# First loads reordered over two queues, VectorE's set-up moved later, the softmax in halves and two expert merges in a row: an attention and expert kernel on one core

## The chip, the core and the metric

The kernel runs on one core of a Trainium2 chip. The core has TensorE (PE: matrix products and transposes, results go to PSUM; its weight loads are listed as PEld), VectorE (DVE), ScalarE (ACT), GpSimd (POOL) and SyncE (SP, which here only issues DMAs). Each engine works through its own list of instructions in order, and the lists meet only at semaphores. The metric is the device time of the program in microseconds (us), lower is better.

## The reference, cut to what matters

```python
# x: 64 sequences x 64 tokens x 256
c = einsum('bsi,bij->bsj', x, weight[ids]) + bias[ids]          # 16 categories, one per sequence
x = x + (c + rezero * lora_linear(attention(c)))                # 16 heads of 16, linear position term, softmax
z = lora_out(x, A[lang], B[lang]) + lang_embed[lang]            # 4 languages, rank 16
ys = geglu(z @ Ws1 + bs1) @ Ws2 + bs2                           # shared expert
top2 of (z @ Wr + br) / 1.5 over 12 experts, softmax of the two # router
x = x + ys + sum over top2 of w * (geglu(z @ We1[e] + be1[e]) @ We2[e] + be2[e])
```

`lora_linear(x)` is `x @ W.T + b + (x @ A.T) @ B.T / 8`, for q, k, v and o.

## The kernel before, in words

The 4096 tokens are 32 tiles of 128 rows (two sequences). Three parts follow each other: an attention part over the 32 tiles (to about 373 us), then the shared expert beside the sorting of tokens to experts, then 75 routed tiles of 128 rows. The change touches the first part alone. The order of the instructions on each engine is written out by hand; nothing plans it.

**Start.** SP issues `load_x(0)`, two of the four projection weights (`wT`, L306), the two category weights and biases of tile 0 (`load_condition`, L289 and L291), the other two `wT` (L310), then tile 1 and the first expert weights. ACT issues four small `low` loads (L515) and ten `first_loads` (L517) on one semaphore. PE runs 40 matmuls on ones (`warm`, L1080), the low-rank products of the projections (L1094), 36 more on ones, `condition(0)` (L1115: c = x times the category weight), `router_rows` (L1085), `c_transpose(0)` (L1122), `project_k`, `project_q` (both L1128), `project_v` (L1147), `condition(1)` and `router_products` (L1103, L1104). DVE first waits for all ten first loads (L672), then runs its set-up (L673 to L688: casts, the language masks, the ones in `vD`, scaled biases), then `c_add(0)` (L709), the four `low_rank_weight` (L695, one for each projection, with L701 for the output's) and `lang_routers` (L768).

**One tile i of attention.** PE: `score(i)` (L1161, L1167), `c_transpose(i+1)` (L1122), `o_transpose(i-1)` (L1197), `low_rank(i-2)` (L1218), `project_k` and `project_q` of i+1 (L1128), `output(i-1)` (L1203), `prob_transpose(i)` (L1175), `row_transpose(i-2)` (L1224), `x2_transpose(i-1)` (L1209), `project_v(i+1)` (L1147), `attend(i)` (L1187), `condition(i+2)` (L1115). DVE: `shift(i)` (the row maximum L735 and its subtraction L739), `k_spread(i+1)` (L714), `t_mask(i-2)` (L796, L797), `x2_add(i-1)` (L764), half of `pT_copy` (L745), `v_spread` (L724), `logit_sum` (L802), `normalize` (L751, L753), `c_add(i+2)` (L709). ACT: `cT_copy` (L533), `oT_copy` (L552), `exps(i)` (L544), `q_copy` (L538), the other half of `pT_copy` (L548), `tT_copy`, `x2T_copy`. POOL: the residual sums and `cut_bias`.

**Merges.** The language part `B` and the first layer of each expert are multiplied into one matrix beforehand. An expert has three units of this (`merge`: 8 weight matmuls L1234 and 16 bias matmuls L1238, into PSUM bank 6, copied out by ACT's L523 and L524). A loop of 12 passes takes two tiles and one expert each. In a pass, unit 0 is merged in the middle of the odd tile (`merge_a`: behind `o_transpose`, in the place of `low_rank`, which then comes behind the projections), unit 1 at the end of the odd tile and unit 2 at the end of the even tile (`merge_b`). Tiles 1 and 2, ahead of the loop, each end with a merge of the shared expert. Tiles 27 to 31, behind it, have none. `logit_consts` (L785, L787) runs once on DVE between tiles 2 and 3.

## Time and profile before

| quantity | value |
|---|---|
| median of 3 runs | 844.94 us (844.64 to 846.51) |
| the profiled execution's own time | 845.6 us |
| its span, first to last instruction | 843.5 us |
| mean granted TensorE clock | 0.992 of full speed |
| PE busy | 811.8 us (96%) |
| DVE busy | 546.8 us (65%) |
| ACT busy | 282.0 us (33%) |
| POOL busy | 406.1 us (48%) |

Times in rows count from the span's start. A timeline row gives the start in us, the length in us, engine and source line, operation, target and sources, how many instructions are put together, and in square brackets how long the engine was idle before it and what it had waited for. PE and PEld overlap: a weight load for the next matmul runs while the present one streams. The engines of one queue run in the written order, so a row that starts late holds up all that stands behind it.

### The profile page before, as it was taken

The page shows a single profiled execution, that of the slowest core. Times are in us where ns is not written, and L with a number is a line of the kernel's source. Part 1 is how long each engine was busy: PE and PEld are TensorE (multiplying, and loading weights), DVE is VectorE, ACT ScalarE, POOL GpSimd, SP SyncE. Part 2 cuts the span into 40 slices and gives each one's busy share as a digit, 9 for nine tenths or more (in the row PEclk, how much of TensorE's full clock was granted, in tenths as well). Part 3 has the DMA queues.
Part 4 walks back from the last instruction along what each step waited for, and adds up shares of the span by engine and source line. Part 5 has one row for each costly group of instructions (what it writes and reads, how often), then busy time and mean ns, then how long its engine had stood idle before and what let it go on. Part 6 is the DMA issues. An engine that isn't in the chain of part 4 may idle for free. (4 is left out here: it accounts for less than half of the span.)

```text
span 843.5 us, 27449 instructions
## 1 busy us (share of the span) xinstructions
PE 811.8 (96%) x9371; PEld 675.0 (80%) x9372; DVE 546.8 (65%) x1231; ACT 282.0 (33%) x783; POOL 406.1 (48%) x511
## 2 busy tenths in 40 slices
PE   6899999999999999979999999999999999999995
PEld 5778888888888888856777888888888888888884
DVE  2586666666666667758887567676676666666662
ACT  0333333333333333433332333232323333332330
POOL 2133333444334444210101277777777777777762
PEclk9999999999999999999999999999999999999998
DMA  9445555555555553103863323222232323232222
GB/s 277 130 137 173 171 161 156 157 167 156 160 168 154 153 158 90 46 2 139 251 209 125 125 34 39 35 35 37 33 39 32 39 33 39 33 38 34 35 34 25
DMA packets 49004, 85.59 MB, mean 101 GB/s; under 512 B 7266, under 2 KB 27554, under 8 KB 48834
## 3 DMA queue, kind: packets, MB, share of 16 engines
q1 hardware_dynamic: 33634, 68.76, 26.2%
q0 software_dynamic: 13888, 15.13, 13.4%
q10 hardware_dynamic: 1440, 1.16, 0.5%
q8 instruction: 23, 0.38, 0.2%
q14 instruction: 19, 0.16, 0.1%
HBM read 68.48 MB, written 16.55 MB: 101 GB/s over the span
## 5 line engine op out<-in xcount | busy, mean ns | idle before, releaser
L1429 PE MATMUL ps<-arena,stage 128*128 x900 | 206.6, 379 | 0.0
L1429 PEld LDWEIGHTS ps<-arena,stage 128*128 128x128 f32 x900 | 165.3, 190 | 19.4
L480 POOL DMA_INDIRECT out_dram<-stage,to_row x75 | 120.6, 1608 | 74.9 <-DVE stage L1040 63.4
L636 ACT ACTIVATE stage<-ps 128x384 f32<-128x384 f32 x150 | 65.4, 488 | 241.6 <-PE ps L1416 241.6
L1416 PE MATMUL ps<-token_rows,token_rows_T 64*128 64x128 f32 x1800 | 129.2, 272 | 0.0
L1416 PEld LDWEIGHTS ps<-token_rows,token_rows_T 64*128 64x128 f32 x1800 | 118.8, 189 | 1.7
L472 POOL DMA_INDIRECT token_rows<-gated_rows,from_row x75 | 75.0, 1000 | 64.6 <-DVE to_row L923 42.0
L388 POOL TENSOR_TENSOR arena<-arena 128x256 f32<-128x256 f32 x32 | 23.3, 729 | 148.7 <-DVE arena L764 148.7
L1014 DVE COPY token_rows<-ps 128x128 f32<-128x128 f32 x75 | 21.8, 291 | 109.6 <-PE ps L1398 109.6
L1024 DVE TENSOR_TENSOR stage<-ps,stage 128x384 f32<-128x384 f32 x150 | 75.8, 547 | 1.8 <-ACT stage L636 1.8
L735 DVE TENSOR_REDUCE arena<-ps 128x16 f32<-128x1024 f32 x32 | 39.2, 1224 | 49.4 <-PE ps L1167 49.2
L1128 PE MATMUL ps<-arena 128*128 128x128 f32 x512 | 66.9, 285 | 1.3 <-ACT arena L533 1.3
L1128 PEld LDWEIGHTS ps<-arena 128*128 128x128 f32 x512 | 61.2, 196 | 4.5 <-issue 2.4
L1410 PE MATMUL ps<-token_rows,token_rows_T 64*128 64x256 bf16 x450 | 62.1, 273 | 0.0
L1327 PE MATMUL ps<-ws,stage 128*128 128x256 f32 x256 | 59.2, 384 | 0.4 <-ACT token_rows_T L560 0.4
L1327 PEld LDWEIGHTS ps<-ws,stage 128*128 128x128 f32 x256 | 47.4, 190 | 10.3 <-issue 4.0
L523 ACT COPY w_merged<-ps 128x256 f32 (+1 forms) x38 | 14.1, 372 | 120.4 <-PE ps L1238 120.4
L267 DVE COPY token_rows_T<-w_merged 128x256 f32 x75 | 46.6, 621 | 0.7 <-issue 0.7
L544 ACT ACTIVATE arena<-arena 128x1024 f32<-128x1024 f32 x32 | 34.0, 1061 | 35.8 <-DVE arena L739 35.8
L1016 DVE TENSOR_SCALAR token_rows<-ps,consts 128x128 bf16<-128x128 f32 x150 | 45.0, 341 | 0.0
L487 POOL COPY token_rows_T<-w_bias 128x384 bf16 x75 | 42.6, 568 | 1.0 <-issue 0.8
L724 DVE TENSOR_TENSOR arena<-ps,arena 64x256 f32<-64x256 f32 x64 | 27.1, 423 | 24.6 <-PE ps L1147 24.2
(170 smaller groups left out, 1482.1 us busy)
## 6 DMA issues: line engine op xcount, KB each, us to landing
stage<-in_we_dram SPq DMA_DIRECT2D x36, 512.0 KB, 4.2
arena<-in_cond_w_dram SPq DMA_DIRECT2D x64, 256.0 KB, 2.9
arena<-in_we_dram SPq DMA_DIRECT2D x12, 768.0 KB, 4.9
arena<-in_x_both_dram SPq DMA_DIRECT2D x32, 256.0 KB, 2.6
arena<-in_L_cond_bias_dram SPq DMA_DIRECT2D x64, 64.0 KB, 2.7
out_dram<-arena SPq DMA_DIRECT2D x32, 128.0 KB, 1.7
be_bc<-in_be_rows_dram SPq DMA_DIRECT2D x13, 192.0 KB, 2.7
gated_rows<-token_rows POOLq DMA_DIRECT2D x2, 1152.0 KB, 10.2
```

The source lines that it names most:

```text
L267: copy(w1x[s % 2][:, j * CW:(j + 1) * CW], w1m[:, ds(e * (NJ * CW) + j * CW, CW)]).then_inc(w1x_ok[j], 1)
L472: pool.indirect_dma_start(s_row[s], None, gated_rows, bass.IndirectOffsetOnAxis(from_row[:, t:t + 1], 0)).then_inc(d_row[s], 16)
L480: pool.indirect_dma_start(out_rows, bass.IndirectOffsetOnAxis(to_row[:, t:t + 1], 0), y_sb[t % YR], None, compute_op=ALU.add).then_inc(d_a ...
L487: nc.gpsimd.tensor_copy(w1bx[t % 2].bitcast(bf16), w1b[:, ds(e * (NJ * P), NJ * P)]).then_inc(w1bx_ok, 1)
L636: nc.scalar.activation(g_sb[hf].rearrange("p (j n) -> p j n", n=P), first_out[1][:, :, hf, :], ACT.Gelu).then_inc(g_ok, 1)
L1016: last = V.tensor_scalar(s_langT[s % 2][:, hf * P:(hf + 1) * P], ps[:, 7, P:2 * P], col["half"][:, hf:hf + 1], None, ALU.mult)
L1024: V.tensor_tensor(actT_sb[s % 2][:, hf, :].rearrange("p (j n) -> p j n", n=P), first_out[0][:, :, hf, :], g_sb[hf].rearrange("p (j n) -> p ...
L1128: last = mm(ps[:, bank, at + m * P:at + (m + 1) * P], wm[w][:, k, m * P:(m + 1) * P], cT[:, k, :], start=(k == 0), stop=(k == KC - 1))
L1327: last = mm(ps[:, 4 + v, half * D:(half + 1) * D], sh_aT[half][:, k, v * P:(v + 1) * P], ws2[:, k, :], start=(k == 0), stop=(k == HS // P ...
L1410: mm(first_out[g][:, j].rearrange("p h n -> p (h n)"), w1bx[s % 2].bitcast(bf16)[64 * g:64 * g + 64, at], s_langT[s % 2][64 * g:64 * g + 6 ...
L1416: last = mm(first_out[g][:, j, hf, :], w1x[s % 2][64 * g:64 * g + 64, j * CW + hf * P:j * CW + (hf + 1) * P], s_rowT[s % 2][64 * g:64 * g ...
L1429: last = mm(ps[:, 4 + s % 2, 0:D], actT_sb[s % 2][:, hf, j * P:(j + 1) * P], arena[:, ds(e * E2 + (NJ * hf + j) * D, D)], start=(hf == 0 a ...
```

## The change

- **Loads.** SP: only the transposed half of tile 0's x, the K weight, the category weights of tile 0 (both value loads first, then both weights, then both biases), the Q weight, the position table (`alibi`), the V weight, tile 1, the output weight, and so on. ACT: four `low`, then the first 132 columns of `consts`, `small`, `bo`, `bv`, the other half of x, and six loads for later (`rest_loads`). The one semaphore of the first loads becomes three (`d_first`, `d_near`, `d_rest`), with one of its own for the half of x. The projections come in the order K, Q, V, output.
- **DVE's set-up.** DVE begins with the K weight and `c_add(0)`. `lang_setup` (the output's weight, `tri`, the language masks, `lang_routers`) stands in tile 0 behind `k_spread(1)`; `langB` is built behind tile 0. On PE `router_rows` moves into tile 0 and `router_products` behind it; 8 `warm` matmuls stand behind `condition(0)`.
- **Waits of other queues.** POOL's `residual(0)` now waits for `s_first` (the scaled `bo`) and comes before the copy of the language masks; SP waits for the pair (`merge_ps`) before it loads units 0 and 1 of the next expert.
- **Softmax in halves.** `shift` and `exps` are each made of two halves of 512 columns, and `prob_transpose` waits for each half.
- **Merges.** Units 0 and 1 are merged together at the end of the odd tile (`merge_pair`, the weights in bank 6, the biases in bank 7), copied by ACT in `pair_bias_copy` and `pair_copy`. The middle of the odd tile has `low_rank` again; in the even tile `o_transpose` waits for `pair_bias` and `low_rank` stands behind the projections. The number of matmuls stays.

```diff
-        first_loads = [
-            (consts[:, :], a["consts"]), (small, a["small"]), (ali_f, a["alibi"]),
-            (aT.rearrange("p c l n -> p (c l n)"), a["lora_aT"]), (a_rows, a["lora_a"]), (ba[:, :, :].rearrange("p c n -> p (c n)"), a["lora_ba"]),
-            (lang_i[:, :], a["lang_of"]), (lang_b[:, :], a["lang_rows"]), (bv_half, a["bv_half"]), (bo_bc, a["bo_rows"])]
-        ALL_FIRST = 16 * len(first_loads)
-        PROJECTIONS = (1, 2, 0, 3)
+        near_loads = [(bo_bc, a["bo_rows"]), (bv_half, a["bv_half"])]
+        rest_loads = [
+            (ba[:, :, :].rearrange("p c n -> p (c n)"), a["lora_ba"]), (consts[:, EARLY:], a["consts"][:, EARLY:]),
+            (lang_i[:, :], a["lang_of"]), (lang_b[:, :], a["lang_rows"]),
+            (a_rows, a["lora_a"]), (aT.rearrange("p c l n -> p (c l n)"), a["lora_aT"])]
+        FIRST, NEAR, REST = 16 * 2, 16 * (len(near_loads) + 1), 16 * len(rest_loads)
+        PROJECTIONS = (1, 0, 2, 3)
...
-            load_x(0, 0)
-            for n in PROJECTIONS[0:2]:
-                sp.dma_start(wm[n].rearrange("p c n -> p (c n)"), a["wT"][n]).then_inc(d_wT[n], 16)
+            sp.dma_start(x_in[0][:, D:2 * D], a["x_both"][0, :, D:2 * D]).then_inc(d_x[0], 16)
+            sp.dma_start(wm[PROJECTIONS[0]].rearrange("p c n -> p (c n)"), a["wT"][PROJECTIONS[0]]
+                         ).then_inc(d_wT[PROJECTIONS[0]], 16)
             sp.wait_ge(d_cat, 16)
             load_condition(0, 0)
-            for n in PROJECTIONS[2:]:
-                sp.dma_start(wm[n].rearrange("p c n -> p (c n)"), a["wT"][n]).then_inc(d_wT[n], 16)
+            n = PROJECTIONS[1]
+            sp.dma_start(wm[n].rearrange("p c n -> p (c n)"), a["wT"][n]).then_inc(d_wT[n], 16)
+            sp.dma_start(ali_f, a["alibi"]).then_inc(d_near, 16)
+            n = PROJECTIONS[2]
+            sp.dma_start(wm[n].rearrange("p c n -> p (c n)"), a["wT"][n]).then_inc(d_wT[n], 16)
+            load_tile(1, True)
+            n = PROJECTIONS[3]
+            sp.dma_start(wm[n].rearrange("p c n -> p (c n)"), a["wT"][n]).then_inc(d_wT[n], 16)
             sp.dma_start(bs2_bc[:, :], a["bs2_rows"]).then_inc(d_bs2, 16)
-            load_tile(1, True)
             for j in range(NJS):
...
-            for dst, src in first_loads:
-                act.dma_start(dst, src).then_inc(d_first, 16)
-
-            def merge_copy(n, j, at_col, summed=None):
+            act.dma_start(consts[:, 0:EARLY], a["consts"][:, 0:EARLY]).then_inc(d_first, 16)
+            act.dma_start(small, a["small"]).then_inc(d_first, 16)
+            for dst, src in near_loads:
+                act.dma_start(dst, src).then_inc(d_near, 16)
+            act.dma_start(x_in[0][:, 0:D], a["x_both"][0, :, 0:D]).then_inc(d_first_x, 16)
+            for dst, src in rest_loads:
+                act.dma_start(dst, src).then_inc(d_rest, 16)
+
+            def merge_copy(n, j, at_col):
                 act.wait_ge(merge_ps, n + 1)
-                if summed is not None:
-                    act.wait_ge(l_sum, summed)
                 copy(w1m[:, ds(at_col, CW)], ps[:, 6, 0:CW])
                 copy(l_ps[:, j * P:(j + 1) * P], ps[:, 6, CW:CW + P]).then_inc(merge_sb, 1)
 
-
-            act.wait_ge(s_sp1, 1)
-            copy(wr[0:NLR + NLANG, :], ps[0:NLR + NLANG, 6, 0:NE]).then_inc(s_sp1c, 1)
-            act.wait_ge(s_hot, 1)
+            def pair_bias_copy(e):
+                act.wait_ge(merge_ps, 2 * e + 3)
+                act.wait_ge(l_sum, e + 1)
+                copy(l_ps[:, 0:2 * P], ps[:, 7, D:D + 2 * P]).then_inc(pair_bias, 1)
+
+            def pair_copy(e):
+                copy(w1m[:, ds(e * (NJ * CW), 2 * CW)], ps[:, 6, 0:2 * CW]).then_inc(merge_sb, 1)
...
             def exps(i):
-                act.wait_ge(shift_sb, i + 1)
-                nc.scalar.activation(probs, probs, ACT.Exp).then_inc(prob_sb, 1)
+                for half in range(2):
+                    act.wait_ge(shift_sb, 2 * i + (half + 1))
+                    part = probs[:, 512 * half:512 * half + 512]
+                    nc.scalar.activation(part, part, ACT.Exp).then_inc(prob_sb, 1)
...
+                tile_steps(i)
+                pair_bias_copy(e)
+                tile_steps(i + 1, pair_of=e, merged=dict(n=2 * e + 3, j=2, at_col=e * (NJ * CW) + 2 * CW))
...
-            dve.wait_ge(d_first, ALL_FIRST)
-            V.tensor_copy(ali, ali_f).then_inc(s_const, 1)
-            V.tensor_copy(tri_b[:, :], col["tri"]).then_inc(s_const, 1)
-            V.tensor_copy(lang_tmp, lang_b[:, :])
-            link(V.tensor_copy(lang_f, lang_i[:, :]))
-            link(V.tensor_scalar(lang_tmp, lang_tmp, col["lang_row"], col["one_row"], ALU.is_equal, ALU.add))
-            for hf in range(2):
-                V.tensor_scalar(langB[:, hf, :], lang_tmp, col["half"][:, hf:hf + 1], None, ALU.mult)
-            for lang in range(NLANG):
-                V.tensor_scalar(lang_hot[:, :, lang], lang_f, float(lang), None, ALU.is_equal)
-            dve.wait_ge(s_zero, 3)
-            for s in range(2):
-                for h in range(2):
-                    V.tensor_copy(vD[s][:, :, :, 32 + h],
-                                  col["kv"][:, h:h + 1].unsqueeze(2).to_broadcast([P, 2, 8]))
-            V.tensor_scalar(bq_quarter, bq_col, 0.25, None, ALU.mult)
-            V.tensor_scalar(bo_rz, bo_bc, rz, None, ALU.mult).then_inc(s_hot, 1)
-            dve.wait_ge(s_hot, 1)
...
             def shift(i):
                 dve.wait_ge(s_ps, i + 1)
-                V.tensor_reduce(smax.rearrange("p (g h) -> p g h", g=4), scores, AX.X, ALU.max).then_inc(max_sb, 1)
-                dve.wait_ge(max_sb, i + 1)
                 if not isinstance(i, int) or i > 0:
                     dve.wait_ge(pT_ps, 2 * i)
-                V.tensor_tensor(probs.rearrange("p (g h k) -> p g h k", g=4, k=S), scores,
-                                smax.rearrange("p (g h) -> p g h", g=4).unsqueeze(3).to_broadcast([P, 4, 4, S]),
-                                ALU.subtract).then_inc(shift_sb, 1)
+                for half in range(2):
+                    banks = slice(2 * half, 2 * half + 2)
+                    top = smax[:, 8 * half:8 * half + 8].rearrange("p (g h) -> p g h", g=2)
+                    V.tensor_reduce(top, scores[:, banks], AX.X, ALU.max).then_inc(max_sb, 1)
+                    dve.wait_ge(max_sb, 2 * i + (half + 1))
+                    V.tensor_tensor(probs[:, 512 * half:512 * half + 512].rearrange("p (g h k) -> p g h k", g=2, k=S),
+                                    scores[:, banks], top.unsqueeze(3).to_broadcast([P, 2, 4, S]),
+                                    ALU.subtract).then_inc(shift_sb, 1)
...
+            def lang_setup():
+                low_rank_weight(3, PROJECTIONS[3])
+                dve.wait_ge(d_rest, REST)
+                V.tensor_copy(tri_b[:, :], col["tri"]).then_inc(s_const, 1)
+                V.tensor_copy(lang_tmp, lang_b[:, :])
+                link(V.tensor_copy(lang_f, lang_i[:, :]))
+                for lang in range(NLANG):
+                    ins = V.tensor_scalar(lang_hot[:, :, lang], lang_f, float(lang), None, ALU.is_equal)
+                ins.then_inc(s_hot, 1)
+                dve.wait_ge(s_hot, 1)
+                lang_routers()
...
+            low_rank_weight(0, PROJECTIONS[0])
             c_add(0, False)
-            for at, n in enumerate(PROJECTIONS):
-                low_rank_weight(at, n)
-            lang_routers()
+            low_rank_weight(1, PROJECTIONS[1])
+            dve.wait_ge(d_first, FIRST)
+            V.tensor_scalar(bq_quarter, bq_col, 0.25, None, ALU.mult).then_inc(s_first, 1)
             k_spread(0)
+            low_rank_weight(2, PROJECTIONS[2])
+            dve.wait_ge(d_near, NEAR)
+            V.tensor_copy(ali, ali_f).then_inc(s_const, 1)
+            V.tensor_scalar(bo_rz, bo_bc, rz, None, ALU.mult).then_inc(s_first, 1)
+            dve.wait_ge(s_zero, 3)
+            for s in range(2):
+                for h in range(2):
+                    V.tensor_copy(vD[s][:, :, :, 32 + h],
+                                  col["kv"][:, h:h + 1].unsqueeze(2).to_broadcast([P, 2, 8]))
             v_spread(0, False)
             c_add(1, True)
-            tile_steps(0, False)
+            tile_steps(0, False, lang_setup)
             router_consts()
+            link(V.tensor_scalar(lang_tmp, lang_tmp, col["lang_row"], col["one_row"], ALU.is_equal, ALU.add))
+            for hf in range(2):
+                V.tensor_scalar(langB[:, hf, :], lang_tmp, col["half"][:, hf:hf + 1], None, ALU.mult)
             tile_steps(1, True)
...
             def prob_transpose(i):
-                pe.wait_ge(prob_sb, i + 1)
                 for n in range(8):
+                    if n % 4 == 0:
+                        pe.wait_ge(prob_sb, 2 * i + (n // 4 + 1))
                     last = tr(ps[:, n // 4, (n % 4) * P:(n % 4 + 1) * P], probs[:, n * P:(n + 1) * P], ident)
...
+            def merge_pair(e, i):
+                for j in range(2):
+                    pe.wait_ge(d_stage[j], 16 * e + 32)
+                pe.wait_ge(tT_sb, i - 1)
+                pe.wait_ge(merge_sb, 2 * e + 2)
+                pe.wait_ge(x2T_sb, i)
+                for j in range(2):
+                    merge_weights(j, j * CW)
+                for j in range(2):
+                    last = merge_biases(j, 7, D + j * P)
...
                 score(i)
                 if one_more:
                     c_transpose(i + 1)
+                if after_pair is not None:
+                    pe.wait_ge(pair_bias, after_pair + 1)
                 if not isinstance(i, int) or i > 0:
                     o_transpose(i - 1)
-                if merge_a:
-                    merge(*merge_a, rows=i - 2 if late else None)
-                elif late:
+                if late and after_pair is None:
                     low_rank(i - 2, merged)
                 if one_more:
                     project_k(i + 1)
                     project_q(i + 1)
-                if merge_a:
+                if late and after_pair is not None:
                     low_rank(i - 2, merged)
+                between()
...
             warm(36)
             condition(0, False)
-            router_rows()
+            warm(8)
+            pe.wait_ge(d_first, FIRST)
             c_transpose(0)
             pe.wait_ge(s_mrgc, 1)
             project_k(0)
+            pe.wait_ge(s_mrgc, 2)
+            project_q(0)
             pe.wait_ge(s_mrgc, 3)
-            project_q(0)
             project_v(0)
             condition(1, True)
-            pe.wait_ge(s_mrgc, 4)
+            pe.wait_ge(s_const, 1)
+            tile_steps(0, False, 0, between=router_rows)
             pe.wait_ge(s_sp1c, 1)
             pe.wait_ge(s_zero, 4)
             router_products()
-            tile_steps(0, False, 0)
-            pe.wait_ge(ar_sb, 1)
-            tile_steps(1, True, 0, merge_b=(0, 0, 16))
-            tile_steps(2, False, 1, merge_b=(1, 1, 16))
+            pe.wait_ge(s_mrgc, 4)
+            tile_steps(1, True, 0, single=(0, 0, 16))
+            tile_steps(2, False, 1, single=(1, 1, 16))
             with pe.Fori(0, NE) as e:
                 i = 2 * e + 3
-                tile_steps(i, True, 3 * e + 3, merge_a=(3 * e + 2, 0, 16 * e + 32), merge_b=(3 * e + 3, 1, 16 * e + 32))
-                tile_steps(i + 1, False, 3 * e + 4, merge_b=(3 * e + 4, 2, 16 * e + 16))
+                tile_steps(i, True, 2 * e + 2, pair=e)
+                tile_steps(i + 1, False, 2 * e + 3, single=(2 * e + 3, 2, 16 * e + 16), after_pair=e)
             for i in range(2 * NE + 3, NT):
                 tile_steps(i, i % 2 == 1, n_merge)
```

## Rows read from the trace of the kernel before

**Rows 1.** Windows of loop tiles: stretch, length, busy PE, PEld, DVE, ACT, POOL, clock, DMA.

```profile
180.44:190.91 10.47, 10.27 (x163) 8.70 (x160) 6.85 (x14) 3.88 (x10) 2.33 (x4) 1.00 0.63 210
190.91:202.74 11.83, 11.80 (x183) 9.69 (x183) 7.03 (x14) 4.43 (x12) 6.81 (x9) 1.00 0.40 119
```

**Rows 2.** Timeline of the start, chain to the first score of tile 0.

```profile
7.39 3.47 PE L1080 MATMUL ps<-ones_b 128*128 128x128 bf16 x36
...
11.78 1.09 PE L1115 MATMUL ps<-arena 128*64 128x256 f32 x8 [0.92 <-DMA arena<-in_cond_w_dram]
...
14.28 0.36 DVE L673 CAST arena<-arena 128x384 bf16<-128x384 f32 x1 [14.15 <-DMA arena<-in_bo_rows_dram]
...
16.78 0.42 DVE L709 TENSOR_TENSOR arena<-ps,arena 128x256 f32<-128x256 f32 x1
...
17.13 2.47 DVE L695 SCALAR_TENSOR_TENSOR arena<-ps,arena 128x512 f32<-128x512 f32 x4
...
18.56 3.75 PE L1128 MATMUL ps<-arena 128*128 128x128 f32 x16 [0.61 <-ACT arena L533]
...
22.25 1.85 PE L1147 MATMUL ps<-arena 128*64 128x128 f32 x16
...
24.91 0.64 PE L1103 MATMUL ps<-arena 64*128 64x48 f32 x4
...
25.83 0.32 PE L1161 MATMUL ps<-arena 2*64 2x256 bf16 x8
```

**Rows 3.** Windows of the start, same columns: the last numbers are clock, DMA share, GB/s.

```profile
17.20:20.00 2.80, 2.12 (x9) 1.75 (x10) 2.77 (x6) 0.37 (x1) 2.06 (x3) 0.50 0.99 372
```

**Rows 4.** DMA issues from 6.50 to 6.70 us (KB, median us to landing).

```profile
arena<-in_wT_dram SPq DMA_DIRECT2D x1, 256.0 KB, 6.4
```

**Rows 5.** Timeline of tile 0 and the start of tile 1, at full clock.

```profile
26.56 0.44 PE L1122 MATMUL ps<-consts,arena 128*128 128x128 f32 x2
...
27.46 2.05 PE L1128 MATMUL ps<-arena 128*128 128x128 f32 x16 [0.46 <-ACT arena L533]
...
31.37 1.15 PE L1147 MATMUL ps<-arena 128*64 128x128 f32 x16
...
32.29 1.13 PE L1187 MATMUL ps<-arena 128*64 128x34 f32 x32
...
35.11 0.32 PE L1161 MATMUL ps<-arena 2*64 2x256 bf16 x8 [0.80 <-DVE arena L778]
```

**Rows 6.** Timeline of one even tile of the loop.

```profile
181.32 1.22 DVE L735 TENSOR_REDUCE arena<-ps 128x16 f32<-128x1024 f32 x1 [1.61 <-PE ps L1167]
...
181.66 0.60 PE L1218 MATMUL ps<-arena 128*128 128x112 f32 x4
...
182.06 1.86 PEld L1128 LDWEIGHTS ps<-arena 128*128 128x128 f32 x16
...
182.67 1.23 DVE L739 TENSOR_TENSOR arena<-ps,arena 128x1024 f32<-128x1024 f32 x1
...
185.02 0.42 DVE L764 TENSOR_TENSOR arena<-ps,arena 128x256 f32<-128x256 f32 x1
185.04 0.86 PEld L1175 LDWEIGHTS ps<-consts,arena 128*128 128x128 f32 x8 [0.46 <-ACT arena L544]
...
185.97 0.25 PEld L1209 LDWEIGHTS ps<-consts,arena 128*128 128x128 f32 x2
```

**Rows 7.** DVE and ACT by form: duration ns min/median/max of 512 and of 1024 columns.

```profile
L745 DVE COPY arena<-ps x32: 690/691/692, 31.5 to 366.4; 128x512 f32<-128x512 f32 x32
...
L544 ACT ACTIVATE arena<-arena x32: 1056/1057/1070, 29.2 to 364.1; 128x1024 f32<-128x1024 f32 x32
```

**Rows 8.** Timeline of tile 3, the first of the loop.

```profile
59.58 1.22 DVE L735 TENSOR_REDUCE arena<-ps 128x16 f32<-128x1024 f32 x1 [0.23 <-DVE logit_consts L787]
...
63.31 1.09 PE L1175 MATMUL ps<-consts,arena 128*128 128x128 f32 x8 [1.70 <-ACT arena L544]
```

**Rows 9.** Timeline of tile 31, the last of the attention part.

```profile
365.23 1.09 PE L1175 MATMUL ps<-consts,arena 128*128 128x128 f32 x8 [1.75 <-ACT arena L544]
```

102 lines of the change are left out of this document (60 added, 42 removed).

## The prediction, made before the changed kernel was run

> **What bounds the kernel now.** I read the busy shares first: PE is busy for 96% of the span (the table above), so time can only come from where PE is idle, where it runs at the lower clock, or where its own order of work has gaps. The windows of single loop tiles come next. In the even tile PE is busy 10.27 of 10.47 us, in the odd one 11.80 of 11.83 [rows 1]: both together hold 0.23 us of idleness in 22.30 us, and 12 passes 2.8 us. This is all that the softmax and the merges can win in the loop, small gaps between groups aside. The start is different: tile 0 is scored at 25.83 us [rows 2], and PE has not done much by then. So I followed the chain to this score, then tiles 0, 1 and 3, where the change adds work to DVE, then one pass, then the end. Sums are made in the profiled execution's time, 845.6 us, which is 0.7 above the median of 844.94.
>
> **The start.** The chain is condition(0), c_add, c_transpose, the projections, condition(1), score [rows 2].
> - Condition(0) waited 0.92 us for a category weight behind the last warm matmul, which ended at 10.86. The new order puts the half of x and one projection weight ahead of it, in place of all of x and two weights, and issues the second category weight right behind the first. It should be there by about 9, so condition(0) runs from 10.86 to 11.95: 0.9 won.
> - DVE's c_add started at 16.78, though condition(0) was done at 12.87: DVE waited for the last first load until 14.28 and then worked 2.5 us on its set-up. Now only the K weight stands before it (2.47 / 4 = 0.62 us, done early), so c_add runs at 12.0 to 12.45. PE spends 8 warm matmuls (8 x 3.47 / 36 = 0.77) beside it, so c_transpose starts at 12.75. At full clock project_k follows c_transpose by 0.90 [rows 5], at 13.65, and both projections take 2.05, to 15.7.
> - V now waits: k_spread(0) until 15.6, the V weight 0.62, project_v at 16.3 for 1.15 [rows 5], condition(1) 1.1 with some overlap, and the score at 18.45. The small pieces of DVE's set-up that stay (position table, scaled `bo`, ones) are about 1.2 us and lie beside project_v. Weights: the third one was issued at 6.6 and landed 6.4 us later, at 13.0 [rows 4]; Q now takes about its place in the bytes, with slightly fewer ahead, and is wanted at 12.45. That is close, and worth 0.5 us if late.
> - The clock: between 17.2 and 20.0 us it was granted at 0.50, the 1.2 GHz level [rows 3], after PE had done next to nothing between 12.87 and 17.2, the end of c_add. There the projections took 3.75 us where they take 2.05 warm, project_v 1.85 where it takes 1.15 [rows 2, 5]. The new gaps are 0.5 to 0.7 us each, far from the 4.3 us of before, so I take the upper level throughout. This is 2.4 us of the sum; if the clock falls all the same, it is lost.
> - The router products (from 24.91 to the score at 25.83, 0.9 us) leave the start.
> Together the score of tile 0 comes at 18.45 in place of 25.83: **7.4 us won**.
>
> **Tiles 0 and 1 give back.** In tile 0 DVE has, from the score on: scores ready 0.9, shift 2.95, k_spread 0.87, the output's weight 0.62 and its scaling 0.5, 7 of 17 set-up instructions (7/17 of 2.5 = 1.0), the routers 0.25, pT_copy 0.69: 7.7. attend needed 6.46 (32.29 - 25.83), now 7.7. Behind it stood 2.82 us to the next score, 0.80 of it a wait for the router constants [rows 5]; now the router products stand there, for about the same. Tile 0: 9.28 becomes 10.5, **1.2 lost**. Everything that queues behind the new waits on DVE (pT_copy, v_spread, normalize) is in this. In tile 1 the constants and langB delay shift by about 0.35, of which 0.1 comes through; tile 2 gives 0.1. The loads of tile 2 wait for POOL's residual(0), now behind the scaled `bo` at about 17.4, against 16.8 before: they are wanted 9 us later.
>
> **Halves.** 512 columns take DVE 0.691 us [rows 7], 1024 take 1.225: a fixed 0.157 us for each instruction. Two more of them, and one more wait for a maximum (0.13 between maximum and subtraction in the loop [rows 6]), less the overlap of one instruction with the next (0.09), lengthen DVE's chain: 1.35 + 1.23 becomes 2.93, **0.35 us more** in each tile. The Trainium skill's "VectorE: DVE Perf Modes" (TRN2 errata) advises tiles of at least 512 elements so that the fixed latency amortizes; halves are just that size. By the rule DVE's chain would not grow; the rows say 23% of a half is fixed. With the rule's reading the total would be some 1.5 us lower. A half of the exponentials takes between 0.53 (half of 1.057) and 0.69 us [rows 7], say 0.6, so the first is ready 1.5 us sooner than all of them were and the second 0.1, and PE's wait before prob_transpose (0.46 on its weight load [rows 6], some 0.25 of real time) goes. What is late next is x2_add. Its end was 4.12 behind the maximum's start (181.32 to 185.44), now 4.47, so x2_transpose can start at 185.85 where it started at 185.97 [rows 6]. **An even tile wins 0.12, not 0.25.**
>
> **Merges in the loop.** The matmuls stay. The odd tile loses the merge in its middle and gets it at its end, where one transition between groups less is worth about 0.1. But that merge covered the exponentials (odd: no idleness) and the cT copy. Odd tile: x2_transpose stood 5.5 into the tile without its merge, and DVE's longer chain also gives 5.55: 11.83 becomes 11.78. Even tile: project_k waits for the cT copy until 182.06 whether low_rank stands ahead of it (from 181.66, about 0.44 until the next group) or not [rows 6], so moving low_rank behind adds 0.44, less the 0.26 of the wait for the exponentials, now covered: 10.47 becomes 10.65. A pass: +0.12. With 12 even and 11 odd tiles (tile 3 is below): **1.5 lost**. Bounds for a pass: -0.33 (all idleness and the transition) to +1.14 (0.44, and 0.35 on both tiles, with nothing won). I take a value near the lower end, since the chain above is made of rows. ACT's copy of the pair's biases (0.37) has 0.9 us until o_transpose. The loads of units 0 and 1 are issued a tile later than before and wanted a pass later.
>
> **Tile 3.** logit_consts holds DVE until 59.58, long after the scores are ready. The merge in the middle lay under this; PE still waited 1.70 [rows 8]. Now the merge comes after: x2_transpose starts at 59.58 + 4.47 + 0.05 = 64.1 (before: 63.31 and the 0.93 from prob_transpose to it in rows 6, 64.2), then 4.7 to the tile's end plus the 1.6 of the second merge: **1.45 lost**. The cover is gone, the stall is not.
>
> **The end.** Tiles 27 to 30 win 0.1 each. In tile 31 PE waits 1.75 for the exponentials [rows 9]; the first four transposes now fall into that wait and the second half is ready a little sooner: 0.6. **1.0 won**. What follows hangs on this chain and shifts as a whole.
>
> **Sum.** 7.4 - 1.2 - 1.5 - 1.45 + 1.0 = 4.2 us: 845.6 becomes 841.4, or 840.7 at the median's level.
>
> **Two queues.** ACT already issued ten loads, so the second queue is not new; what changes is order and bytes. "DMA: Bandwidth & Descriptors" of the Trainium skill (Rules for kernel authors) says that spreading loads over queues gives no bandwidth. The gain above counts none from it; nothing in the traces here can part the two.
>
> **Rivals.**
> - *The clock falls at the start.* The two gaps before and after the projections join if Q or V land late. For it: at 12.87 a gap did it. Against: PE is busy for most of 10.9 to 18.5. It costs 2.4: 843.1.
> - *The loop wins.* If x2_add turns out to be no limit and the pair saves two transitions, a pass wins 0.2: 12 x 0.32 better than forecast, 836.9. For it: the margins are 0.1 us. Against: in rows 6 DVE's chain is that close to PE.
> - *The loop loses, slower in all.* The place is the even tile's projections and the x2_transpose of both tiles: without the merge in the middle nothing lies beside cT copy and softmax, and the longer DVE chain comes through whole. At the upper bound, 1.14 a pass, the loop costs 13.7 in place of 1.5: 852.9. It makes the change slower by over 0.2% from 0.62 a pass on. Against: PE has 5.5 us of its own work before x2_transpose. A part of it, 0.4 a pass, gives 844.1.
> - *The change does not do what it says:* condition(0) still finds its weight late and Q's weight at 13.0. That takes back 1.4: 842.1.
>
> **How the numbers follow.** A measurement here tells 0.2%, 1.7 us. Forecast 840.7 with its near neighbours (839 to 842): 0.50. Loads not earlier: 0.06, faster. Loop wins: 0.15, faster. Cold start: 0.11, on the edge at 843.1; I give 0.04 to faster and 0.07 to same. Loop loses in part: 0.11, same. Loop loses in full: 0.07, slower. Faster 0.75, same 0.18, slower 0.07. The range from 836.5 to 844.5 leaves out the slower case and a part of the partial one.
>
> **What would show it.** Right: score(0) near 18.5 and the clock at 1.00 from 11 us on; attend(0) waiting for DVE; score(1) near 29; tile 3 near 15 us long; a pass of 22.4; in the even tile a wait for ACT before project_k; no wait before prob_transpose. Wrong: a clock of 0.50 before 25 us; a pass under 22.1 or over 22.7; PE waiting for `pair_bias`; a shift of DVE longer than 2.95.

## The result, and the profile after

The changed kernel takes 834.83 us (median of 4 runs, 834.17 to 835.57) where the one before takes 845.04 (4 runs): a ratio of 0.9874, with a 95% interval of 0.9861 to 0.9888. That is 10.2 us faster. The forecast was 840.7, 4.2 us faster, with a range down to 836.5, so the direction was right and the forecast size was less than half of what came. The profiled execution took 834.26 us, with a span of 832.0, 11.5 below the span of before.

Busy time of each engine, from the page of the changed kernel:

```profile
span 832.0 us, 27568 instructions
...
PE 802.4 (96%) x9379; PEld 677.4 (81%) x9380; DVE 551.5 (66%) x1295; ACT 285.6 (34%) x791; POOL 406.1 (49%) x511
```

DVE is busy for 4.7 us more than before; with the halves alone (run h_only below) it is 3.6 us more. PE is busy for 9.4 us less with 8 more matmuls. Some 2.1 us of this are the matmuls on ones, the projections and project_v of the start (rows below). For the rest, busy time is what the overlapping records cover together, and it gets smaller when they lie closer.

The start of the changed kernel (timeline: start, length, engine and line, operation, count, in brackets the idle time before). L1114 are the matmuls on ones, L1149 condition, L714 c_add, L1162 the projections, L1181 project_v, L1195 the score.

```profile
6.78 2.18 PE L1114 MATMUL ps<-ones_b 128*128 128x128 bf16 x36
...
8.90 1.09 PE L1149 MATMUL ps<-arena 128*64 128x256 f32 x8
...
10.99 0.42 DVE L714 TENSOR_TENSOR arena<-ps,arena 128x256 f32<-128x256 f32 x1 [3.42 <-DMA arena<-in_L_cond_bias_dram]
...
12.52 3.38 PE L1162 MATMUL ps<-arena 128*128 128x128 f32 x16 [0.55 <-DVE arena L700]
...
15.83 1.38 PE L1181 MATMUL ps<-arena 128*64 128x128 f32 x16
...
18.00 0.32 PE L1195 MATMUL ps<-arena 2*64 2x256 bf16 x8
```

They answer to rows 2. Condition(0) starts 2.9 us sooner, c_add 5.8 sooner and the score 7.8 sooner. The matmuls on ones took 2.18 us where they took 3.47 for the same 36. The projections still took 3.38 us, at a granted clock of 0.50 from about 13 to 16 us.

Windows of an odd and an even tile of the loop and of tile 3 (stretch, length, busy PE, PEld, DVE, ACT, POOL, clock, DMA share, GB/s), against rows 1:

```profile
161.01:172.29 11.28, 11.28 (x184) 9.98 (x185) 6.97 (x16) 4.08 (x11) 6.77 (x9) 1.00 0.45 152
172.29:182.95 10.66, 10.25 (x164) 8.76 (x160) 7.07 (x16) 4.43 (x12) 2.33 (x4) 1.00 0.59 184
48.00:62.54 14.54, 11.94 (x188) 9.89 (x184) 10.90 (x19) 4.04 (x11) 6.34 (x9) 1.00 0.34 108
```

The odd tile got shorter by 0.55 us and the even one longer by 0.19, as had been worked out for the even one (10.65). Taken as means of eleven passes, a pass went from 22.27 to 21.92. From the starts of the scores in both timelines the 11.5 us divide as follows (positive: won).

| stretch | forecast | measured |
|---|---|---|
| start to score(0) | 7.4 | 7.8 |
| tile 0 | -1.2 | -0.9 |
| tiles 1 and 2 | 0 | 0.4 |
| tile 3 | -1.45 | -0.9 |
| score(4) to score(27) | -1.5 | 3.7 |
| score(27) to the end | 1.0 | 1.4 |

The forecast of this sum was 4.2 us and it came to 11.5. The loop carries 5.2 of the missing 7.3 us; the other five lines came out 0.3 to 0.55 better each.

### The profile page after: what moved, and what is told of

Read it like the earlier page. It is cut to its first block, busy times and chain, and to the rows that moved or that the text cites. A ratio compares the mean times of both kernels' runs of the same rounds, so it can differ in the third digit from the quotient of the medians.

```text
span 832.0 us, 27568 instructions
## 1 busy us (share of the span) xinstructions
PE 802.4 (96%) x9379; PEld 677.4 (81%) x9380; DVE 551.5 (66%) x1295; ACT 285.6 (34%) x791; POOL 406.1 (49%) x511
## 4 chain that ended last, share of the span: by engine, by line
PE 92%; DVE 3%; issue 1%; ACT 1%; DMA 1%; SPq 1%; POOL 0%; DVEq 0%
PE ps L1490 23%; PE ps L1477 12%; PE ps L1162 7%; PE ps L1388 7%; PE ps L1181 4%; PE ps L1471 4%; PE ps L1264 4%; PE ps L1210 3%; PE ps L1222 3%; PE ps L1238 3%; PE ps L1149 3%; PE ps L1377 3%; PE ps L1270 2%; PE ps L1458 2%; PE ps L1201 2%; PE ps L1253 2%
## 5 line engine op out<-in xcount | busy, mean ns | idle before, releaser
L745 DVE TENSOR_REDUCE arena<-ps 128x8 f32<-128x512 f32 x64 | 43.8, 685 | 64.4 <-PE ps L1201 64.1
L1162 PE MATMUL ps<-arena 128*128 128x128 f32 x512 | 66.5, 284 | 4.2 <-ACT arena L552 3.6
L1162 PEld LDWEIGHTS ps<-arena 128*128 128x128 f32 x512 | 60.8, 195 | 7.7 <-ACT arena L552 7.0
L565 ACT ACTIVATE arena<-arena 128x512 f32<-128x512 f32 x64 | 40.4, 631 | 38.2 <-DVE arena L747 37.1
L747 DVE TENSOR_TENSOR arena<-ps,arena 128x512 f32<-128x512 f32 x64 | 44.2, 691 | 2.2
L1471 PEld LDWEIGHTS ps<-token_rows,token_rows_T 64*128 64x128 bf16 x450 | 22.2, 95 | 24.9 <-issue 24.9
```

What stands on the lines that cost most here:

```text
L747: V.tensor_tensor(probs[:, 512 * half:512 * half + 512].rearrange("p (g h k) -> p g h k", g=2, k=S), scores[:, banks], top.unsqueeze(3).to ...
L1162: last = mm(ps[:, bank, at + m * P:at + (m + 1) * P], wm[w][:, k, m * P:(m + 1) * P], cT[:, k, :], start=(k == 0), stop=(k == KC - 1))
L1471: mm(first_out[g][:, j].rearrange("p h n -> p (h n)"), w1bx[s % 2].bitcast(bf16)[64 * g:64 * g + 64, at], s_langT[s % 2][64 * g:64 * g + 6 ...
```

## The experiments

All times are medians; a ratio is to the kernel before on the same chip, and comparisons between sets go by ratios, because the kernel before took 845.8, 846.0, 846.7 and 847.3 us in the four sets. Starts of scores come from the timelines. A trace shows one execution, and not always a typical one, which matters where the clock fell in it.

**1. The three parts alone.** Each is the kernel before with one part of the change: `shift`, `exps` and `prob_transpose` in halves; the pair with its copies, waits and counts; or everything else.

```diff
-                V.tensor_reduce(smax..., scores, AX.X, ALU.max)
+                for half in range(2):
+                    V.tensor_reduce(top, scores[:, banks], AX.X, ALU.max)
```

> The kernel before with the softmax in halves and nothing else. Theory A (in the loop PE only loses its wait for the exponentials, and x2_add is no limit, since DVE's chain grows by 0.16 us and not by 0.35): the even tile falls from 10.47 to about 10.22, the odd one stays at 11.83, tiles 27 to 30 win 0.15 to 0.2 each and tile 31 0.6: about 4 us in all, 841. Theory B (the loop's gain in the changed kernel comes from the pair, halves give the 0.12 an even tile that was forecast): 2.4 us, 842.6.

Measured: 839.16 us, ratio 0.9918 (0.9905 to 0.9932), 6.6 us won. The two tiles of a pass:

```profile
155.84:166.06 10.22, 10.05 (x164) 8.80 (x160) 6.96 (x16) 4.11 (x12) 2.33 (x4) 1.00 0.69 212
166.06:177.87 11.81, 11.81 (x185) 9.66 (x186) 7.26 (x16) 4.51 (x13) 6.79 (x9) 1.00 0.44 122
```

The even tile is where theory A put it, at 10.22, but the whole is 2.6 us more than the 4 of theory A. Its trace is 6.0 us shorter than the one before: 3.1 from score(4) to score(27), 1.4 in tiles 0 to 3, where theory A counted nothing, and 1.5 behind score(27). DVE's part of this even tile:

```profile
156.81 0.69 DVE L742 TENSOR_REDUCE arena<-ps 128x8 f32<-128x512 f32 x1 [1.71 <-PE ps L1172]
...
157.54 0.69 DVE L744 TENSOR_TENSOR arena<-ps,arena 128x512 f32<-128x512 f32 x1
...
158.15 0.68 DVE L742 TENSOR_REDUCE arena<-ps 128x8 f32<-128x512 f32 x1
...
158.86 0.69 DVE L744 TENSOR_TENSOR arena<-ps,arena 128x512 f32<-128x512 f32 x1
...
160.56 0.41 DVE L769 TENSOR_TENSOR arena<-ps,arena 128x256 f32<-128x256 f32 x1
```

The four pieces take 2.74 us (156.81 to 159.55), against 2.58 before (181.32 to 183.90 in rows 6). The 0.13 between maximum and subtraction became 0.04 and 0.03. x2_add ends 4.16 after the first maximum, against 4.12 before.

That 0.13 was never a cost of the two operations. In the kernel before it is 0.13 to 0.14 in the 24 tiles of the loop, but 0.03 to 0.04 in the eight tiles outside it, as here in tile 0:

```profile
26.72 1.23 DVE L735 TENSOR_REDUCE arena<-ps 128x16 f32<-128x1024 f32 x1 [1.27 <-PE ps L1167]
27.98 1.23 DVE L739 TENSOR_TENSOR arena<-ps,arena 128x1024 f32<-128x1024 f32 x1
```

With the halves it is 0.03 to 0.04 in all 32 tiles. The code of the halves puts the wait for `pT_ps` ahead of the first maximum, where it stood between maximum and subtraction. That this is what took the 0.10 is likely but was not run by itself.

```diff
-                tile_steps(i, True, 3 * e + 3, merge_a=(3 * e + 2, 0, ...), merge_b=(3 * e + 3, 1, ...))
-                tile_steps(i + 1, False, 3 * e + 4, merge_b=(3 * e + 4, 2, ...))
+                tile_steps(i, True, 2 * e + 2, pair=e)
+                tile_steps(i + 1, False, 2 * e + 3, single=(2 * e + 3, 2, ...), after_pair=e)
```

> The kernel before with units 0 and 1 merged as a pair at the end of the odd tile and nothing else. Theory A (a second merge behind the first costs 1.3 us in place of 1.6, but the odd tile now waits for the exponentials, 0.26, and the even one for the cT copy): a pass of about 22.2 for 22.31, and tile 3 about 1 us longer: 844.5, within 1 us of before. Theory B (the pair carries the loop's gain): a pass of 21.95, 3.5 us in all, 841.5. Theory C, the forecast's own sizes (+0.12 a pass with halves, more without): 847 or slower.

Measured: 848.51 us (10 runs, 847.6 to 850.7), ratio 1.0033 (1.0022 to 1.0044): 2.8 us slower. A pass:

```profile
161.97:172.64 10.67, 10.26 (x163) 8.77 (x160) 6.93 (x14) 4.22 (x11) 2.32 (x4) 1.00 0.55 185
172.64:184.32 11.68, 11.63 (x185) 9.98 (x185) 6.84 (x14) 3.87 (x10) 6.77 (x9) 1.00 0.47 145
```

As means of eleven passes the odd tile is 11.64, the even one 10.65 and a pass 22.28, against 22.27 before, so the pair alone does nothing in the loop. Tile 3 takes 14.92 for 13.62. This explains 1.3 of the 2.8 us. The time is that of theory C (847 or slower), but not by its reason, since the pass did not grow; theory A had the loop and tile 3 right and the time wrong. The profiled execution was the slowest of the ten (850.66). It shows the clock at 0.50 around 372 us and 1.1 us more behind score(27), and a start 2.5 us later in front of which nothing was changed. How much of the rest the clock makes is not settled.

```diff
-            dve.wait_ge(d_first, ALL_FIRST)
-            (the set-up, then c_add(0), the four weights, lang_routers)
+            low_rank_weight(0, PROJECTIONS[0])
+            c_add(0, False)
+            (as in the change)
```

> The kernel before with the new order of the loads and of DVE's set-up and nothing else. Both theories: score(1) at about 28 for 35.1, tiles 1 to 31 as before: 7 us, 838. If the start's gain were given back later or were a matter of the clock's phase at the start, it would be under 5 us, 840 or more, with a wide spread of the times.

Measured: 839.09 us, ratio 0.9923 (0.991 to 0.9937), 6.7 us won; score(0) at 18.72, score(1) at 28.62. The start keeps what it wins. But not all else is as before: from score(4) to score(27) this kernel is 0.9 us faster too. The first eight matmuls of each pass take 0.32 us, where they take 0.46 in the kernel before, and the odd tile is 11.70 for 11.79; why is not shown. The three parts alone sum to 6.6 - 2.8 + 6.7 = 10.5 us, about what they make together.

**2. Order inside the pair.**

```diff
                 for j in range(2):
                     merge_weights(j, j * CW)
-                for j in range(2):
                     last = merge_biases(j, 7, D + j * P)
```

> The changed kernel with the matmuls of a pair in the order weights, biases, weights, biases in place of weights, weights, biases, biases. The same matmuls, two more changes of the matmul's tile shape in each pass. If such a change costs PE about 0.15 us (a matmul row of 8 weights starts the next group after 1.02 us alone and 0.86 as a second one), a pass is 0.3 longer, 12 passes 3.5 us: 838.3. If changes of shape are free and the pass is shorter for another reason (no wait, the start of the loop body): no difference, 834.8.

Measured: 838.8 us, ratio 0.9913, against 0.9874 of the changed kernel (0.9883 when run again): about 3 us slower. As means of eleven passes, a pass went from 21.92 to 22.21, all of it in the odd tile (11.28 to 11.56), which is 3.1 us from score(4) to score(27). The merges of the changed kernel and, below, of this one (timeline, PE):

```profile
169.40 1.95 PE L1264 MATMUL ps<-stage,ba 128*64 128x256 f32 x16
...
171.28 1.08 PE L1270 MATMUL ps<-stage,ba 128*32 128x128 f32 x32
...
172.29 0.32 PE L1195 MATMUL ps<-arena 2*64 2x256 bf16 x8
```

```profile
149.62 1.08 PE L1264 MATMUL ps<-stage,ba 128*64 128x256 f32 x8
150.63 0.64 PE L1270 MATMUL ps<-stage,ba 128*32 128x128 f32 x16
151.21 1.08 PE L1264 MATMUL ps<-stage,ba 128*64 128x256 f32 x8
152.22 0.64 PE L1270 MATMUL ps<-stage,ba 128*32 128x128 f32 x16
152.79 0.32 PE L1195 MATMUL ps<-arena 2*64 2x256 bf16 x8
```

The same 48 matmuls take 2.89 us in one order (169.40 to 172.29) and 3.17 in the other. Two more changes from one kind of matmul to the other cost 0.28, 0.14 each. The two kinds differ in the tile's shape, in the columns that they stream (256 and 128) and in the PSUM bank that they write. From weights to biases the bank is not what counts: in the kernel before both kinds write bank 6, and the two groups together take the same 1.59 us. Shape and columns were not parted.

**3. The changed kernel with one part less, and again.** The kernels of this set ran beside each other.

> The changed kernel once more, as the measure for the kernels of this set: about 10.5 us under the kernel before, 835 on a chip where that takes 845.5. In its trace passes of 21.94 and tile 3 of 14.5.

Measured: 836.19 us, ratio 0.9883 (0.9867 to 0.99). Its tile 3 took 16.09 us where the first profile had 14.54. Windows inside it:

```profile
52.00:54.00 2.00, 0.62 (x3) 0.19 (x1) 1.63 (x4) 0.12 (x1) 1.15 (x2) 1.00 0.03 12
54.00:56.00 2.00, 0.77 (x5) 0.54 (x6) 1.97 (x6) 1.31 (x4) 0.00 (x0) 1.00 0.01 4
56.00:58.00 2.00, 2.00 (x15) 1.55 (x16) 1.27 (x4) 1.42 (x5) 1.19 (x2) 0.72 0.00 0
58.00:60.00 2.00, 2.00 (x34) 2.00 (x32) 0.83 (x2) 0.00 (x0) 1.13 (x3) 0.50 0.61 139
```

PE is busy for 1.39 of 4 us while it waits for the late exponentials, then the clock falls to the 1.2 GHz level from about 57 to 60 us, and the tile is 1.55 us longer. The first profile shows the same gap (PE busy for 1.40 of the 4 us) and a clock of 1.00 throughout the tile. So the gap brings the fall in some executions and not in others: of the seven profiles of kernels with the pair and with `logit_consts` in one piece five have it in tile 3, and of the nine others none.

```diff
-                tile_steps(i, True, 2 * e + 2, pair=e)
+                tile_steps(i, True, 3 * e + 3, merge_a=(3 * e + 2, 0, ...), merge_b=(3 * e + 3, 1, ...))
```

> The changed kernel with the three merges where they were before (start and halves kept). Theory A' (from the traces of the single parts: with halves alone a pass is 22.03 and tile 3 13.2, with all three 21.94 and 14.5; the pair wins 12 x 0.09 and gives 1.3 back at tile 3): no difference to the changed kernel, within 0.5 us. Theory B' (the times, in which the pair alone made the kernel before 2.8 us slower, hold here too): 2 us or more faster than the changed kernel.

Measured: 832.51 us, ratio 0.984 (0.9826 to 0.9855): 3.7 us faster than the changed kernel beside it. Theory A' missed, theory B' held. A pass and tile 3:

```profile
148.71:158.97 10.26, 10.05 (x163) 8.80 (x160) 6.97 (x16) 4.14 (x12) 2.33 (x4) 1.00 0.68 217
158.97:170.68 11.71, 11.71 (x185) 9.62 (x185) 7.26 (x16) 4.47 (x13) 6.81 (x9) 1.00 0.40 116
47.61:60.85 13.24, 12.36 (x187) 9.51 (x184) 10.90 (x19) 4.58 (x13) 6.32 (x9) 1.00 0.33 98
```

The passes are equal, 21.97 here and 21.94 with the pair (21.92 for both as means). At score(4) this kernel is already 3.3 us ahead (60.85 for 64.17), 2.85 of them from tile 3: 1.3 because the merge lies inside the wait again (13.24 for 14.54) and 1.55 because the clock did not fall.

```diff
-                for half in range(2):
+                V.tensor_reduce(smax..., scores, AX.X, ALU.max)      (exps and prob_transpose likewise)
```

> The changed kernel with the softmax whole (start and pair kept). Theory A': a pass goes back to 22.28, the odd tile waits 0.3 for the exponentials; tiles 27 to 31 give back 1.2; 12 x 0.34 + 1.2 and some tenths for tiles 1 to 3: about 5.8 us slower than the changed kernel, near 841. If the halves' worth in the kernel before (6.6) was there because nothing else covered the exponentials, and the pair had taken a part of it: 3 us or less.

Measured: 842.2 us (839.2 to 844.3), ratio 0.9943 (0.9926 to 0.9961): 6.0 us slower, as expected. The halves are worth about the same with the pair as without, but in another tile. Here the odd tile is 11.56 and the even one 10.66, as means; with the halves they are 11.28 and 10.65. Without the pair the halves shorten the even tile (10.49 to 10.21) and leave the odd one alone (11.79 and 11.81).

```diff
+            logit_consts(0)
             tile_steps(2, False)
-            logit_consts()
+            logit_consts(NT // 2)
```

> The changed kernel with logit_consts cut in two: its first half (2.5 us on DVE) between tiles 1 and 2, its second between tiles 2 and 3. Theory A' (tile 3 takes 14.5 and not 11.3 since DVE comes to its scores 3.4 us late and the merge that lay beside this is now behind it): each half makes the shift 0.9 us late at most, PE has 5.3 us of its own work before x2_transpose and DVE 4.2, so tile 3 falls to 11.3 to 11.6 and tile 2 grows by 0.2 at most: 3 us faster than the changed kernel. If the cover is not the cause (a first pass of a loop is slow for another reason): no gain.

Measured: 832.27 us, ratio 0.9839 (0.9821 to 0.9858): 3.9 us faster than the changed kernel. Tile 3, at full clock:

```profile
48.53:60.57 12.04, 11.73 (x188) 9.98 (x185) 8.46 (x17) 4.04 (x11) 5.63 (x9) 1.00 0.38 124
```

It falls to 12.04, not quite to the 11.3 to 11.6 that were expected, and tile 2 grows from 9.98 to 10.43. By the traces this is 2.1 us against an execution of the changed kernel without the fall of the clock, and 3.6 against the one with it. So the long wait at tile 3, with the fall that it brings in some executions, is what makes the pair cost: the pair's 3.7 us come back when the wait is cut short with the pair in place.

**4. What the start's gain is made of.**

```diff
-            (loads as changed)
+            (both halves of x, two projection weights, category weights and biases, two projection weights; ACT: consts in two pieces, ..., bo last)
```

> The changed kernel with the loads issued in the order of before (both halves of x, two projection weights, category weights and biases by turns, alibi third and bo last on ACT's queue, consts whole at once in two pieces); DVE's set-up, softmax and merges as changed. Theory 1 (the start's gain comes mostly from c_add no longer standing behind DVE's set-up and the last load): condition(0) waits for the category weight until about 11.8 and c_add runs at 13, score(0) at about 20 for 18.0: 2 us slower than the changed kernel, 837.5 or so. Theory 2 (the order of the loads carries it): score(0) at 22 or later, 4 us slower or more.

Measured: 835.76 us (835.1 to 839.3), ratio 0.987 (0.9851 to 0.9889), the same as the changed kernel. By the median both theories missed. The edit differs from its description in one point: inside `load_condition` the order stayed that of the change (both weights, then both biases), so this order was not taken back. The one profiled execution took 839.32, with the clock at 0.50 from 12 to 18 us and again in tile 3:

```profile
11.40 1.59 PE L1149 MATMUL ps<-arena 128*64 128x256 f32 x8 [2.90 <-DMA arena<-in_cond_w_dram]
...
14.94 3.75 PE L1162 MATMUL ps<-arena 128*128 128x128 f32 x16 [0.55 <-ACT arena L552]
```

Here condition(0) starts 2.5 us later than in the changed kernel, and score(0), at 20.59, 2.6 later, as theory 1 had it. The other three executions, between 835.1 and 836.2, have no trace; their mean granted clocks (0.996, 0.996, 0.992) are above the 0.990 of the profiled one and reach above the 0.992 to 0.994 of the changed kernel in the second set. So fewer falls of the clock may hide a cost of the old order, and this stays open.

```diff
+            dve.wait_ge(d_rest, REST)
+            dve.wait_ge(d_near, NEAR)
             low_rank_weight(0, PROJECTIONS[0])
```

> The changed kernel, but DVE's first instruction waits until all first loads have landed (about 14 us), as before the change; the set-up itself stays moved. Theory 1: c_add at 14.6 for 11.0, and the clock falls in the longer gap of PE: score(0) at 22.5, 4.5 us slower than the changed kernel. Theory 2: the wait is covered by loads that come late anyway: 2 us or less.

Measured: 840.85 us, ratio 0.9936 (0.9921 to 0.9952): about 5 us slower than the changed kernel by the ratios. Score(0) is at 22.18, and the wait shows:

```profile
14.24 0.69 DVE L700 SCALAR_TENSOR_TENSOR arena<-ps,arena 128x512 f32<-128x512 f32 x1 [14.11 <-DMA arena<-in_lora_aT_dram]
...
15.41 0.66 PE L1158 MATMUL ps<-consts,arena 128*128 128x128 f32 x2 [4.91 <-DVE arena L714]
```

Score(0) comes 4.2 us later than in the changed kernel, of the 7.8 that the start had won: more than half of the start's gain is that DVE no longer waits for loads that it doesn't need yet. What the order of the loads is worth the medians do not show. The moved set-up was not run by itself.

**5. Better versions.**

```diff
                 for b, cat in enumerate(cats):
-                    (category weight)
+                    (category bias)
...
             c_transpose(0)
+            warm(5)
...
             project_q(0)
+            warm(8)
```

> The changed kernel with logit_consts cut in two (between tiles 1 and 2, and 2 and 3), the category biases issued ahead of the category weights, and 13 more matmuls on ones in PE's two waits among the projections of tile 0. Against logit_split (832.3) the c_add of tile 0 comes 0.9 us earlier, of which 0.5 reach score(0), since condition(1) waits for its weights at 16: 831.8. If the extra matmuls delay PE rather than keep its clock: 832.3 or more.

Measured: 834.2 us (831.3 to 835.7), ratio 0.9846 (0.9825 to 0.9867). The 831.8 was missed.

> The same, but with the merges where they were before the change. If the pair is worth nothing in the loop (passes of 21.94 with it and 21.92 without) and the split removes what it costs at tile 3, this is the same as best_pair within 0.5 us. If the pair is still a cost: 1 us or more faster than best_pair.

Measured: 833.42 us, ratio 0.9846 (0.9829 to 0.9863). The two are alike, but neither beats logit_split (0.9839). The early biases don't bring the 0.9 us:

```profile
11.36 1.93 PE L1149 MATMUL ps<-arena 128*64 128x256 f32 x8 [3.05 <-DMA arena<-in_cond_w_dram]
```

This row is from best_pair. The category weights, issued 1.5 us later behind the biases, now make condition(0) start at 11.36 for 8.90 (11.03 in best_no_pair): score(0) is at 19.9 and 19.4. So the two kernels without the early biases were run:

> The changed kernel with the merges where they were before the change and logit_consts cut in two; the loads as changed. Theory A' (the pair wins nothing in the loop and costs 1.3 us at tile 3 by its place behind the tile, which the split takes away): the same as logit_split, 0.984 of the kernel before, since both then have passes of 21.9 and no long gap at tile 3; tile 3 about 11.8. If the pair costs something besides tile 3: clearly below, 0.982 or less.

Measured: 831.72 us (830.3 to 835.7), ratio 0.9809 (0.9795 to 0.9822), **the lowest ratio of all, 15.6 us under the kernel before it ran with**. Tile 3 takes 11.70, as an odd tile of its loop does; with the pair (logit_split) it takes 12.04 where the loop's odd tile is 11.28. Against logit_split the ratio is 0.003 lower, with intervals that just touch, in different sets; the traces have tiles 2 and 3 at 22.24 here and 22.46 there and equal passes. By the number this is the second case of the expectation, by the traces the first, so whether the pair costs anything besides tile 3 stays open.

> The same with 13 more matmuls on ones in PE's two waits among the projections of tile 0 (5 behind c_transpose(0), 8 behind project_q(0)). Theory: in some executions the clock is at 0.50 from 12 to 16 us after PE's waits for c_add and for the weights; the extra matmuls are too few and too late for that, since the fall comes before them: no difference to split_no_pair, within 0.5 us. If they keep the clock up: 1 us faster, and the spread of the times narrower.

Measured: 831.86 us (830.6 to 832.9), ratio 0.9816 (0.9802 to 0.9829): no difference. The profiled execution has the clock at 1.00 all through the start, that of split_no_pair has it at 0.50 from 14 to 18 us, and the projections take 2.02 here and 3.75 there. In the medians this does not show. Its start, at full clock:

```profile
12.73 2.02 PE L1159 MATMUL ps<-arena 128*128 128x128 f32 x16 [0.27 <-ACT arena L546]
...
16.80 1.09 PE L1146 MATMUL ps<-arena 128*64 128x256 f32 x8 [0.23 <-issue]
```

The second row is condition(1), and score(0) follows at 17.82. The changed kernel, with its projections 1.4 us longer, had it at 18.00.

## Why the prediction was wrong

**The direction held, and with it most steps outside the loop.** The start was forecast at 7.4 and gave 7.8, tile 0 at 1.2 and gave 0.9 back, the even tile at 10.65 and was 10.66, the end at 1.0 and was 1.4. The step that failed is the pass of the loop, forecast at +0.12 and measured at -0.36 (22.30 to 21.94), and in it the odd tile: "11.83 becomes 11.78", and it became 11.28. Two signs named as wrong came, a pass under 22.1 and a clock of 0.50 before 25 us. The rows of an odd tile, before and after, with merge, projections and x2_transpose:

```profile
192.35 1.08 PE L1234 MATMUL ps<-stage,ba 128*64 128x256 f32 x8
193.37 0.64 PE L1238 MATMUL ps<-stage,ba 128*32 128x128 f32 x16
193.94 2.05 PE L1128 MATMUL ps<-arena 128*128 128x128 f32 x16
...
198.12 0.38 PE L1209 MATMUL ps<-consts,arena 128*128 128x128 f32 x2
```

```profile
166.37 0.38 PE L1244 MATMUL ps<-consts,arena 128*128 128x128 f32 x2
```

By the forecast's own numbers x2_transpose stands 5.55 into the tile, the end of the first merge 4.7 later, and the second merge takes 1.5. Measured are 5.36 (161.01 to 166.37), 4.62 and 1.30. Two terms were mis-sized and one was missing.

**"DVE's longer chain also gives 5.55", "0.35 us more".** The gap of 0.13 between maximum and subtraction, read from the loop, was charged to both halves. 0.04 and 0.03 were left, the shift grew by 0.16, and the chain up to the end of x2_add by 0.04 (4.12 to 4.16). Tile 0 of the kernel before has a gap of 0.03, which would have warned. Most of the other 0.12 had been slack: before, x2_add started 0.30 after t_mask's last operation had started, and with the halves 0.19 after it. Before, the output matmuls that it needs ended only then:

```profile
183.96 1.03 PE L1203 MATMUL ps<-arena 128*128 128x256 f32 x4
```

So the halves' gain came through to x2_transpose in whole. Without the halves it stands 5.64 into the odd tile, with them 5.36, and the odd tile goes from 11.56 to 11.28. In the kernel before, where the merge covers the odd tile's exponentials, the same 0.28 is won in the even tile, where 0.12 was forecast. PE's idle time in a window had been taken as a limit of what can be won, and it is none: in that even tile PE shows 0.05 us of idleness before prob_transpose (its weight load 0.46), and the halves brought x2_transpose 0.28 earlier.

The forecast's sentence that goes by the 512-element advice of "VectorE: DVE Perf Modes" of the Trainium skill (TRN2 errata), and lets DVE's chain not grow, came nearer to the time than the sum did, by luck. That page of the Trainium skill speaks of operands in SBUF, and these operations read PSUM. The trace does not bear out that the fixed part of an instruction goes away at this size: each half took 0.69 us where the whole took 1.22. What went is the gap.

**"One transition between groups less is worth about 0.1".** It is the size of the second merge. Behind a first one it takes 1.30 us (2.89 - 1.59), not 1.5, because the weights of both and the biases of both follow each other; the other order, w, b, w, b, costs the difference again (run pair_wbwb). The merge in the middle of the odd tile also had gaps of 0.17 and 0.20 on the weight load at its two ends, which went with it.

**The missing term** is the 0.1 us of the first eight matmuls of a pass, which came with the loads and the set-up (run s_only) and whose cause is open.

**The even tile** came out as forecast and by the forecast's mechanism. In the changed kernel project_k waits for the cT copy with nothing in front of it, and low_rank, behind the projections, covers the exponentials, so the halves win nothing there (10.66 without them, 10.65 with them):

```profile
173.91 2.05 PE L1162 MATMUL ps<-arena 128*128 128x128 f32 x16 [0.24 <-ACT arena L552]
```

The pair thus costs the even tile 0.16 and gives the odd one 0.16 (11.79 to 11.64): by itself it is worth nothing in the loop, as p_only and no_pair say. The loop's gain is the halves' (0.26 a pass in h_only) and the 0.1.

**Tile 3** was the right mechanism: the cover gone, the stall not. Its size was 0.9 in the first profile and 2.5 in the second, where the clock fell. The forecast had weighed a fall of the clock only at the start, though it had worked out itself that PE would wait longest here. The first profile was an execution without the fall, and the medians lie about 1 us nearer to the kernel before than the profiles do.

**The start** came out right in its size, but not step by step, and in part by luck. The forecast put condition(0) at 10.86, behind matmuls on ones whose 3.47 us were read from one execution; in the profiles of the changed kernel and of all 14 experiments they took 2.18, and condition(0) started at 8.90 in the changed one. The gain ended at the category biases, for which c_add waited until 10.99, still 1 us before the forecast; the forecast never asked when they come. And the clock did fall, from about 13 to 16 us (0.50), against the forecast, which made the projections 1.4 us longer. That did not cost score(0) the 1.4: in four profiles without the fall it came at 17.61 to 18.08, since PE there waited for the V weight (0.2 to 0.7 us) and then before condition(1), which started 0.1 us after its second weight load had landed (at 16.5 to 17.0). A longer fall, in split_no_pair, did cost: score(0) at 20.01. The next limit of the start is tile 1's category weights, which the forecast did not name.

**Of the rivals** "the loop wins" is nearest to what happened, with 836.9 against 834.8 measured. Its price, 0.2 a pass, was about half of what came, and it had been given 0.15. Its first reason (x2_add is no limit) was right. Its second (the pair saves transitions) was right for the odd tile, but the even tile takes the saving back. The bound for a pass, -0.33, was built on PE's idle time, and the measured -0.36 lies beyond it.

## What to carry to other kernels

A wait at the head of an engine's list should cover the next instruction's needs and no more: taking DVE's first wait for all ten loads away was worth 4 to 5 us here. The worth of the order of the loads could not be told from the medians, though one misplaced pair of loads moved the first matmuls by over 2 us. Work that is moved out of a stall leaves the stall behind: look for every place where it was the cover, once-only places outside the steady state too, and shorten the stall itself (cutting `logit_consts` in two won back the 3.7 us that moving the merge had lost). Keep matmuls of one kind together, and cut a long vector operation when the next engine can start on a half. Before a gap between two instructions is charged as their cost, look at the same pair in another place.

## What the runs showed of the hardware that was not expected

- Under 3 us of idleness of PE, in pieces, is enough for the clock to fall in some executions: in tile 3 of the changed kernel PE was busy for 1.39 of 4 us, and the clock then stood at 0.50 from about 57 to 60 us in one profile and stayed at 1.00 in another of the same kernel.
- The first matmuls of an execution have long weight loads (151 ns median in the kernel before, 98 in the changed one, for the same instruction, with a granted clock of 1.00 in the rows), and when they become short differs between executions.
- A change between two kinds of matmul (tiles of 64 output columns of the array that stream 256 columns, tiles of 32 that stream 128) cost PE 0.14 us each.
- The gap between two dependent instructions of DVE (the row maximum and its subtraction) was 0.13 to 0.14 us in the 24 loop tiles of the kernel before, 0.03 to 0.04 in its eight tiles outside the loop, and 0.03 to 0.04 everywhere with the halves.
- Two loads of 64 KB ahead of two of 256 KB delayed the start of condition(0) by 2.1 to 2.5 us. Of this 1.5 us is the later issue of the larger ones; where the rest comes from is not shown.
